# ScalarE's order at the end of an attention batch: two value chunks taken ahead of a weight unit's high half

## The chip, the core and the metric

The program runs on one core of a Trainium2 chip. The metric is device time in microseconds (us) of one execution. The core has TensorE (PE, with its weight loads shown apart as PEld), VectorE (DVE), ScalarE (ACT), GpSimd (POOL) and SyncE (SP), each with its own queue of instructions that runs in order and waits on semaphores. In the profile, PEclk is the TensorE clock that was granted, where 1.00 is 2.4 GHz and 0.50 is 1.2 GHz.

## The reference

For 4 batches of 512 tokens of width 256: layer norm, one attention head of width 256 over a context of 512 rows of width 192, a residual; then layer norm, a router that picks 2 of 8 experts per token, and a residual.

```
x = x + xattn(layernorm(x), ctx, Wq, bq, Wk, bk, Wv, bv)      # softmax(q k^T / 16) v
x = x + ffn(layernorm(x), Wr, W1, b1, W2, b2)
# ffn: probs = softmax(x Wr^T); the top 2 of 8, renormalised to w
#      out += (gelu(x W1[e]^T + b1[e]) W2[e]^T + b2[e]) * w_e      for each expert e
```

## The kernel before

The kernel has an attention phase, up to about 138 us, and an expert phase behind it, in which PE is busy nearly all the time with fp16 matmuls. The experts' fp32 weights are 16 units (W1 and W2 of 8 experts). They are loaded and split into a high and a low fp16 half during the attention phase, in the gaps of its engines. For each unit `u` the steps are:

- SP loads it into one of the staging buffers (`load_unit`, line 368). For a buffer that was used before, it first waits for the low half of the earlier unit (line 372).
- ACT squares it and sums it up (`square`, 852, the instruction is line 856). PE adds the sums over partitions (`add_all`, 691), two units at a time.
- DVE makes the scale factors out of that sum (`scale`, 1097: the first instruction, line 1105, reads the sum's PSUM bank and frees it, line 1112 writes `up`).
- ACT writes the high half (`high`, 859, line 861, 128x2048 elements). It waits for the factors (`scale_ready`).
- DVE writes the low half out of the staged unit and the high half (`low`, 1116, line 1121, two instructions of 128x1024). It waits for the high half (`high_ready`).

The attention of a batch `b` goes in four tiles of 128 queries: scores on PE (line 637) into `s_ps`, negated row maximum on DVE (`row_max`, line 1079), exponential on ACT (line 841), a transpose on PE (line 647) that ACT takes to SBUF (line 849), the product with the values on PE (`attend`, line 656), the residual on DVE (line 1092).

Projections and the small matmuls of the router share two PSUM banks, `proj0` and `proj1`, in a fixed order of uses (`projection_order`, line 111). Use n goes to bank n % 2, and PE waits in `begin` (line 571) until use n - 2 was taken. At the end of a batch the uses are the sum of two units (`sum`, taken by DVE's line 1105), and then the four chunks of the next batch's values (`v` 0 to 3, two matmuls each, shown as four), taken by ACT at line 832. So chunk 1 needs the bank of the sum, chunk 2 that of chunk 0, and chunk 3 that of chunk 1.

The order of the work is written by hand, engine by engine. At the end of batch b, with u = 4b, it reads (b from 0 to 2):

- PE: `attend(b, 2)`, the sum, `attend(b, 3)`, the four value chunks, then for batch b+1 `scores` 0 and 1, the sum of units u+4 and u+5, the transposes of `xn2` (`turn_normal`, line 611, two banks, the second of which waits until DVE has read that sum), the transpose of the first probabilities, `scores` 2, the logits.
- ACT: `square(u + 4)`, `high(u + 2)`, `values(b + 1)`, `high(u + 3)`, the store, `square(u + 5)`, then the first two exponentials of batch b+1.
- DVE (from line 1339): `scale(2b + 1)`, the last residual, the moments of the second layer norm (lines 1021, 1024), `low(u + 2)`, in batch 2 a table of 16 small instructions (`first_table`, 1194), `ln2_apply(b)` (line 1028), `rows_high` (line 1069), then for batch b+1 `row_max` 0, half of `low(u + 3)`, `row_max` 1, `scale(2b + 2)`.
- POOL: four indirect DMAs (line 516) that scatter rows of batch b-1, then the power that gives `rstd` for `ln2_apply` (line 503), then four more such DMAs.

Of the kernel before, what the change touches and what calls it, by code (L numbers as in the profile page):

```python
# [36 lines left out]
KT = LK // P  # L37
# [105 lines left out]
def build(nc, x, ctxT, WqT, bq, WkT, WvB, WrT, W1T, b1, W2T, b2, rows, out):  # L143
    uses = projection_order()
    with ExitStack() as ctx:
# [198 lines left out]
        def bank_of(*use):  # L344
            return proj[uses[use] % 2]

        def unit_tiles(u):

            e = u // 2
            return (w1h[:, e, :], w1l[:, e, :]) if u % 2 == 0 else (w2h[:, e, :], w2l[:, e, :])  # L350
# [471 lines left out]
        def _(act):  # L822
# [3 lines left out]
            def take(use, out_ap, in_ap, bias=None, scale=1.0):  # L826
                n = uses[use]
                if taken_by_vector(use):
                    return
                act.wait_ge(proj_full, n + 1)  # L830
                if bias is None:
                    nc.scalar.activation(out_ap, in_ap, ACT.Copy, scale=scale).then_inc(proj_free[n % 2], 1)
                else:
                    nc.scalar.activation(out_ap, in_ap, ACT.Identity, bias=bias, scale=scale).then_inc(proj_free[n % 2], 1)

            def soft(b, q):
                n = QT * b + q
                act.wait_ge(max_ready, n + 1)
                if n >= 2:
                    act.wait_ge(t_full, n - 1)  # L840
                nc.scalar.activation(probs[:, n % 2, :], s_ps[n % 2][:, 0:LK], ACT.Exp, bias=negmax[:, n:n + 1],
                                     accum_out=rowsum[:, n:n + 1]).then_inc(p_ready, 1)

            def take_turned(b, q):
                n = QT * b + q
                act.wait_ge(t_full, n + 1)
                if n >= 2:
                    act.wait_ge(o_full, n - 1)
                nc.scalar.activation(probsT[:, n % 2, :, :].rearrange("p a b -> p (a b)"), t_ps[n % 2][:],
                                     ACT.Copy).then_inc(pt_ready, 1)  # L850

            def square(u):


                act.wait_ge(staged_in[STAGE[u]], 16 * STAGE[0:u + 1].count(STAGE[u]))
                nc.scalar.activation(unit_tiles(u)[u < UNITS - 1].bitcast(BF16), stages[STAGE[u]], ACT.Square,
                                     accum_out=sq[:, u, 0:1]).then_inc(squared, 1)

            def high(u):
                act.wait_ge(scale_ready, u // 2 + 1)  # L860
                nc.scalar.activation(unit_tiles(u)[0], stages[STAGE[u]], ACT.Copy,
                                     scale=up[:, u, 0:1].bitcast(F32)).then_inc(high_ready, 1)
# [2 lines left out]
                for c in range(DC):  # L865
                    take(("a", 0, c), a_sb[:, c, 0:FEAT], bank_of("a", 0, c)[:, 0:FEAT])

            def values(b):
                for k in range(KT):
                    take(("v", b, k), v_sb[:, k, :], bank_of("v", b, k)[:, 0:D])  # L870

            def queries(b):
                for c in range(2):
                    take(("q", b, c), qT[0:PART[c], c, :], bank_of("q", b, c)[0:PART[c], 0:LQ],
                         bias=qb_sb[0:PART[c], c:c + 1], scale=SCALE)

            def turned_rows(name, b):
                for c in range(DC):
                    take((name, b, c), normT[:, c, :], bank_of(name, b, c)[:])

            def store(b):

                act.wait_ge(x2_ready, QT * (b + 1))
                if b:
                    act.wait_ge(stored, 16 * b)
                act.dma_start(out[b * LQ:(b + 1) * LQ, :].rearrange("(t p) d -> p t d", p=P),
                              x_sb[b % XBUF]).then_inc(stored, 16)

            def take_logits(b):
                take(("logits", b, 0), lg[:].rearrange("p a b -> p (a b)"), bank_of("logits", b, 0)[:, 0:QT * E])  # L890
# [8 lines left out]
            for b in range(B):  # L899
                u = QT * b  # L900
                last = b == B - 1
                soft(b, 0)
                if not b:
                    high(0)
                soft(b, 1)
                if b:
                    turned_rows("x2t", b - 1)
                take_turned(b, 0)
                if last:
                    square(u + 2)  # L910
                elif b:
                    high(u)
                else:
                    high(1)
                if b:
                    take_logits(b - 1)
                soft(b, 2)
                take_turned(b, 1)
                if last:

                    act.wait_ge(xn_ready, B)
                    act.wait_ge(proj_full, uses["xt", B - 1, 1] + 1)
                    square(u + 3)
                else:
                    square(u + 2)
                if b and not last:
                    high(u + 1)
                soft(b, 3)
                if not last:
                    turned_rows("xt", b + 1)  # L930
                take_turned(b, 2)
                if not last:
                    square(u + 3)
                    queries(b + 1)
                else:
                    high(u)
                take_turned(b, 3)
                if last:
                    high(u + 1)

                    act.wait_ge(stored, 16 * (B - 1))
                else:
                    square(u + 4)
                high(u + 2)
                if not last:
                    values(b + 1)
                high(u + 3)
                store(b)
                if not last:
                    square(u + 5)  # L950
# [529 lines left out]
```

## Time and profile before

| what | value |
|---|---|
| median of 3 runs | 376.73 us (376.52 to 377.44) |
| span of the profiled execution, first to last instruction | 373.9 us |
| PE, DVE, ACT, POOL busy | 336.9, 272.9, 189.5, 122.7 us |
| mean granted TensorE clock | 0.973 |

The profile gives the span of its execution and no other time of it; the median of the runs is 2.8 us above the span, for what lies ahead of the first and behind the last instruction. A busy share says how long an engine had work under way, and not whether the end of the kernel waited for it. For that there is the chain of waits, which is followed back from the last instruction. In the timeline a row is a start, a duration, an engine, a line and what is written out of what; "x8" is a count of merged instructions, and the bracket at its end is the engine's idle time before the row, with what ended it.

### The profile page before, as it was taken

What the parts mean: (1) busy time and instruction counts of PE and PEld (TensorE: products, weight loads), DVE (VectorE), ACT (ScalarE), POOL (GpSimd) and SP (SyncE); (2) the same over time, 40 slices, a digit from 0 to 9 for tenths busy, and PEclk for the clock granted to TensorE, in tenths of its full rate; (3) what the DMA queues carried; (4) which work ended last, traced back from release to release, by engine and by line L of the source; (5) the groups of instructions that cost most, each with busy time, mean ns of one, the idle gap of its engine ahead of it and who ended that gap; (6) DMA issues with size and microseconds to landing.
All of it is one profiled execution on the core that took longest, in us unless ns stands there. A gap on an engine that the chain in (4) does not pass through costs nothing.

```text
span 373.9 us, 8773 instructions
## 1 busy us (share of the span) xinstructions
PE 336.9 (90%) x2657; PEld 271.2 (73%) x2657; DVE 272.9 (73%) x753; ACT 189.5 (51%) x333; POOL 122.7 (33%) x124
## 2 busy tenths in 40 slices
PE   8998999789977849898699999999999999999980
PEld 4555765557645638787488888889898889988860
DVE  4259788987998699988777776756577776757760
ACT  2587798578577766171333334434454443445300
POOL 5017102382182173027623212233423132241322
PEclk9999999999989999999699999999999999999996
DMA  7977871465357326223425333434234333434312
GB/s 258 365 267 234 305 257 66 141 238 173 127 178 239 104 84 203 43 33 116 83 32 87 54 48 44 58 44 59 39 51 56 48 45 59 58 42 54 37 16 28
DMA packets 51112, 41.82 MB, mean 112 GB/s; under 512 B 28541, under 2 KB 46526, under 8 KB 50942
## 3 DMA queue, kind: packets, MB, share of 16 engines
q1 hardware_dynamic: 40798, 27.36, 26.0%
q0 software_dynamic: 7872, 11.77, 17.3%
q10 hardware_dynamic: 2400, 2.13, 1.7%
q8 instruction: 26, 0.43, 0.5%
q14 instruction: 16, 0.13, 0.1%
HBM read 22.28 MB, written 13.86 MB: 97 GB/s over the span
## 4 chain that ended last, share of the span: by engine, by line
PE 71%; DVE 16%; issue 5%; POOL 3%; ACT 1%; DMA 1%; POOLq 1%; DVEq 0%; SPq 0%; ACTq 0%
PE o_ps L781 26%; PE s_ps L763 15%; PE t_ps L763 13%; PE s_ps L637 3%; PE proj L624 3%; PE o_ps L656 3%; DVE w2l L1121 2%; DVE w1l L1121 2%; POOL rstd L503 2%; PE proj L603 2%; DVE negmax L1079 2%; PE o_ps L570 1%; PE proj L611 1%; POOL rows L516 1%; PE t_ps L647 1%
## 5 line engine op out<-in xcount | busy, mean ns | idle before, releaser
L548 POOL DMA_INDIRECT out<-y,xm x39 | 61.3, 1573 | 129.3 <-DVE y L1392 122.5
L969 ACT ACTIVATE g<-s_ps,b_sb,down 128x256 f32<-128x256 f32 (+1 forms) x100 | 45.4, 519 | 82.7 <-PE s_ps L763 72.2
L781 PE MATMUL o_ps<-w2h,gh 128*128 x312 | 85.0, 272 | 0.0
L781 PE MATMUL o_ps<-w2h,gl 128*128 x312 | 85.0, 272 | 0.0
L781 PE MATMUL o_ps<-w2l,gh 128*128 x312 | 85.0, 272 | 0.0
L1365 DVE TENSOR_SCALAR gh<-g,up 128x512 f16<-128x512 f32 x78 | 38.2, 489 | 36.5 <-ACT g L969 33.6
L969 ACT ACTIVATE g<-t_ps,b_sb,down 128x256 f32<-128x256 f32 (+1 forms) x92 | 42.3, 524 | 39.0 <-PE t_ps L763 38.6
L1367 DVE SCALAR_TENSOR_TENSOR gl<-g,up,gh 128x512 f16<-128x512 f32 x78 | 58.6, 752 | 2.8
L763 PE MATMUL s_ps<-xT,w1h 128*128 128x256 f16 (+1 forms) x400 | 52.3, 256 | 7.3 <-DVE w2l L1121 4.9
L763 PE MATMUL t_ps<-xT,w1h 128*128 128x256 f16 (+1 forms) x368 | 50.2, 261 | 0.8 <-issue 0.8
L516 POOL DMA_INDIRECT rows<-send,place x32 | 35.6, 1112 | 32.9 <-DVE place L1186 24.6
L763 PEld LDWEIGHTS s_ps<-xT,w1h 128*128 x400 | 35.0, 100 | 12.0 <-issue 8.6
L763 PEld LDWEIGHTS t_ps<-xT,w1h 128*128 x368 | 32.9, 100 | 7.0 <-issue 2.5
L763 PE MATMUL s_ps<-xT,w1l 128*128 128x256 f16 (+1 forms) x200 | 35.0, 256 | 2.9 <-issue 2.9
L781 PEld LDWEIGHTS o_ps<-w2h,gh 128*128 128x128 f16 x312 | 30.5, 98 | 4.4 <-issue 0.2
L781 PEld LDWEIGHTS o_ps<-w2l,gh 128*128 128x128 f16 x312 | 30.5, 98 | 3.8
L781 PEld LDWEIGHTS o_ps<-w2h,gl 128*128 128x128 f16 x312 | 30.5, 98 | 3.4
L763 PE MATMUL t_ps<-xT,w1l 128*128 128x256 f16 (+1 forms) x184 | 32.6, 259 | 0.0
L656 PE MATMUL o_ps<-v_sb,probsT 128*128 128x256 f32 x128 | 30.5, 383 | 0.0
L1388 DVE SCALAR_TENSOR_TENSOR y<-o_ps,undo,b_sb 128x256 f32<-128x256 f32 x39 | 18.9, 484 | 15.1 <-PE o_ps L781 8.6
L503 POOL TENSOR_TENSOR rstd<-vare,half 128x4 f32<-128x4 f32 x8 | 10.6, 1328 | 44.9 <-DVE vare L1024 44.9
L656 PEld LDWEIGHTS o_ps<-v_sb,probsT 128*128 128x128 f32 x128 | 23.1, 190 | 2.6
(231 smaller groups left out, 505.6 us busy)
## 6 DMA issues: line engine op xcount, KB each, us to landing
staged<-W2T SPq DMA_DIRECT2D x8, 1024.0 KB, 6.8
staged<-W1T SPq DMA_DIRECT2D x7, 1024.0 KB, 4.9
rows<-send POOLq DMA_DIRECT2D x8, 260.0 KB, 4.0
x_own<-x SPq DMA_DIRECT2D x2, 512.0 KB, 5.4
w2l<-W1T SPq DMA_DIRECT2D x1, 1024.0 KB, 10.3
out<-x_own ACTq DMA_DIRECT2D x2, 512.0 KB
b_sb<-b SPq DMA_DIRECT2D x1, 1024.0 KB, 5.5
out<-y,xm POOLq DMA_INDIRECT x39, 3.8
```

Of the source, the lines that this page charges most:

```text
L503: nc.gpsimd.tensor_tensor(rstd[:, which, b * QT:(b + 1) * QT], vare[:, which, b * QT:(b + 1) * QT], half[:, b * QT:(b + 1) * QT], ALU.pow) ...
L516: pool.indirect_dma_start(out=rows, out_offset=bass.IndirectOffsetOnAxis(ap=place[:, b, k, q:q + 1], axis=0), in_=send[b % 2][:, q, :], in ...
L548: pool.indirect_dma_start(out=out, out_offset=bass.IndirectOffsetOnAxis(ap=xm[:, t % MB, r, META - 1:META].bitcast(I32), axis=0), in_=y2[: ...
L624: i = nc.tensor.matmul(bank[0:PART[c], 0:LQ], a_sb[:, t, c * P:c * P + PART[c]], normT[:, t, :], start=(t == 0), stop=(t == DC - 1))
L656: i = nc.tensor.matmul(o_ps[n % 2][:, 0:D], probsT[:, n % 2, k, :], v_sb[:, k, :], start=(k == 0), stop=(k == KT - 1))
L763: i = nc.tensor.matmul(h_ps[group % 4][:, to:to + width(t)], w[:, bass.ds(e, 1), at:at + P].rearrange("p a n -> p (a n)"), xT[:, t % XB, x ...
L781: i = nc.tensor.matmul(y_ps[n % 2][:, 0:D], l[:, t % 2, m, r * P:(r + 1) * P], w[:, bass.ds(e, 1), m * D:(m + 1) * D].rearrange("p a n -> ...
L969: i = nc.scalar.activation(g[:, m, 0:width(t)], h_ps[group % 4][:, at:at + width(t)], ACT.Gelu, bias=b1_sb[:, bass.ds(e, 1), m:m + 1].rear ...
L1121: i = nc.vector.scalar_tensor_tensor(out=lo[:, n], in0=stages[STAGE[u]][:, n], scalar=up[:, u, 0:1].bitcast(F32), in1=hi[:, n], op0=ALU.mu ...
L1365: nc.vector.tensor_scalar(gh[:, t % 2, m, n], g[:, m, n], by, None, ALU.mult).then_inc(g_high, 1)
L1367: nc.vector.scalar_tensor_tensor(out=gl[:, t % 2, m, n], in0=g[:, m, n], scalar=by, in1=gh[:, t % 2, m, n], op0=ALU.mult, op1=ALU.subtract ...
L1388: nc.vector.scalar_tensor_tensor(out=y1[:, r, :], in0=y_ps[(BEFORE[t] + r) % 2][:, 0:D], scalar=undo[:, bass.ds(e, 1)], in1=b2_sb[:, bass. ...
```

## The change

ACT takes chunks 0 and 1 of the next batch's values ahead of `high(u + 2)`, and chunks 2 and 3 behind it, where all four stood behind it. That is at the end of batches 0, 1 and 2. No instruction is added or removed, and the orders of PE, DVE, POOL and SP stay as they are.

```
-            def values(b):
-                for k in range(KT):
+            def values(b, chunks):
+                for k in chunks:
                     take(("v", b, k), v_sb[:, k, :], bank_of("v", b, k)[:, 0:D])
...
                 else:
                     square(u + 4)
+                if not last:
+                    values(b + 1, range(0, 2))
                 high(u + 2)
                 if not last:
-                    values(b + 1)
+                    values(b + 1, range(2, KT))
                 high(u + 3)
                 store(b)
```

ScalarE's instructions at the end of batch 0, before (-) and now (+). `v_sb` holds the values, `w1h` is the high half of unit 2, `w2h` that of unit 3, and the line with `sq` is `square(4)`:

```order
 L849 ACTIVATE probsT<-t_ps 128x512
 L856 ACTIVATE w1l,sq<-w2l 128x2048
-L861 ACTIVATE w1h<-staged,up 128x2048
-L832 ACTIVATE v_sb<-proj 128x256 x4
+L832 ACTIVATE v_sb<-proj 128x256 x2
+L861 ACTIVATE w1h<-staged,up 128x2048
+L832 ACTIVATE v_sb<-proj 128x256 x2
 L861 ACTIVATE w2h<-staged,up 128x2048
 L886 DMA out<-x_own 128x4x256
```

Two of the four takes moved ahead of the high half of unit 2.

ScalarE's instructions at the end of batch 2, where `w1h` is the high half of unit 10, `w2h` that of unit 11, and the line with `sq` is `square(12)`:

```order
 L849 ACTIVATE probsT<-t_ps 128x512
 L856 ACTIVATE w1l,sq<-staged 128x2048
-L861 ACTIVATE w1h<-staged,up 128x2048
-L832 ACTIVATE v_sb<-proj 128x256 x4
+L832 ACTIVATE v_sb<-proj 128x256 x2
+L861 ACTIVATE w1h<-staged,up 128x2048
+L832 ACTIVATE v_sb<-proj 128x256 x2
 L861 ACTIVATE w2h<-staged,up 128x2048
 L886 DMA out<-w1h 128x4x256
```

The same two takes moved; at the end of batch 1 it is the same again.

## Rows read from the trace of the kernel before

**Rows 1.** The page: the chain that ended last, share of the span by engine.
```profile
PE 71%; DVE 16%; issue 5%; POOL 3%; ACT 1%; DMA 1%; POOLq 1%; DVEq 0%; SPq 0%; ACTq 0%
```

**Rows 2.** Timeline, end of batch 0, ACT and PE.
```profile
40.76 1.90 PE L603 MATMUL proj<-w1l,w2l 128*128 128x256 f32 x8
40.80 2.00 ACT L861 ACTIVATE w1h<-staged,up 128x2048 f16<-128x2048 f32 x1 [0.90 <-DVE up L1112]
...
42.71 0.64 ACT L832 ACTIVATE v_sb<-proj 128x256 f32<-128x256 f32 x2
...
43.12 2.00 PE L603 MATMUL proj<-w1l,w2l 128*128 128x256 f32 x8 [0.47 <-ACT v_sb L832]
44.29 0.38 ACT L832 ACTIVATE v_sb<-proj 128x256 f32<-128x256 f32 x1 [0.95 <-PE proj L603]
```

**Rows 3.** Timeline, end of batch 0, DVE.
```profile
42.83 2.48 DVE L1121 SCALAR_TENSOR_TENSOR w1l<-staged,up,w1h 128x1024 f16<-128x1024 f32 x2 [0.20 <-ACT w1h L861]
45.23 1.38 DVE L1028 TENSOR_SCALAR xn<-x_own,mv,rstd 128x256 f32<-128x256 f32 x4
...
49.05 0.68 DVE L1079 TENSOR_REDUCE negmax<-s_ps 128x1 f32<-128x512 f32 x1
49.80 0.16 DVE L1105 COPY total<-proj 128x4 f32<-128x4 f32 x1
```

**Rows 4.** Chain in order of time, first scores of batch 1: start, us, what.
```profile
50.69 0.44 PE t_ps L647 x4
51.13 1.73 PE s_ps L637 x4
```

**Rows 5.** Timeline, end of batch 1.
```profile
71.58 1.13 PE L603 MATMUL proj<-w1l,w1h 128*128 128x256 f32 x4 [0.39 <-DVE total L1105]
...
74.27 2.48 DVE L1121 SCALAR_TENSOR_TENSOR w1l<-staged,up,w1h 128x1024 f16<-128x1024 f32 x2
74.56 2.00 PE L603 MATMUL proj<-w1l,w1h 128*128 128x256 f32 x8 [1.85 <-issue]
74.67 1.72 POOL L516 DMA_INDIRECT rows<-send,place  x1 [0.30 <-issue]
...
76.40 1.25 POOL L503 TENSOR_TENSOR rstd<-vare,half 128x4 f32<-128x4 f32 x1
...
77.69 1.41 DVE L1028 TENSOR_SCALAR xn<-w2h,mv,rstd 128x256 f32<-128x256 f32 x4 [0.94 <-POOL rstd L503]
```

**Rows 6.** Timeline, end of batch 2.
```profile
103.92 1.13 PE L603 MATMUL proj<-w1l,w2l 128*128 128x256 f32 x4 [0.39 <-DVE total L1105]
...
104.61 2.00 ACT L861 ACTIVATE w1h<-staged,up 128x2048 f16<-128x2048 f32 x1
...
105.65 0.96 POOL L516 DMA_INDIRECT rows<-send,place  x1 [0.30 <-issue]
...
106.65 2.48 DVE L1121 SCALAR_TENSOR_TENSOR w1l<-staged,up,w1h 128x1024 f16<-128x1024 f32 x2
...
106.94 3.11 PE L603 MATMUL proj<-w1l,w2l 128*128 128x256 f32 x8 [1.89 <-issue]
...
109.84 4.22 PE L637 MATMUL s_ps<-w2l,qT 128*128 128x512 f32 x8
...
116.83 0.66 PE L611 MATMUL proj<-ident,xn 128*128 128x128 f32 x4 [1.66 <-DVE total L1105]
```

**Rows 7.** Windows: stretch, its length, each engine's busy time, PEclk, DMA.
```profile
103.53:107.68 4.15, 1.87 (x7) 1.36 (x8) 3.81 (x16) 3.63 (x5) 3.24 (x4) 1.00 0.77 277
107.68:111.09 3.41, 3.41 (x8) 2.36 (x7) 3.10 (x14) 1.39 (x3) 3.19 (x3) 0.50 0.28 56
...
116.83:125.31 8.48, 8.48 (x46) 6.30 (x47) 4.72 (x12) 6.10 (x12) 0.00 (x0) 1.00 0.45 140
133.20:138.16 4.96, 0.02 (x1) 0.00 (x1) 4.85 (x9) 2.86 (x2) 4.04 (x4) 1.00 0.21 75
138.40:141.81 3.41, 3.41 (x34) 3.38 (x33) 3.31 (x9) 1.49 (x2) 2.71 (x3) 0.50 0.72 242
```

## The prediction

> **What bounds the kernel now.** I read the page's chain first. PE holds 71% of it and DVE 16% [rows 1], but that is a mean over two phases, and the change lies in the first, the attention phase up to 138 us. So I read the chain in order of time there, and then the timeline at the ends of batches 0, 1 and 2. The reader is to look at who waits for whom at these three places.
>
> At the end of batch 0, PE waits 0.47 us at chunk 2 of the values until ACT has taken chunk 0, which stands behind the high half of unit 2 [rows 2]. At the end of batches 1 and 2 the same wait is 1.85 and 1.89 us [rows 5, 6]. The page calls these two "issue"; the order of the code names the take of chunk 0 as what PE lacks. These are the waits that the change takes away, 4.2 us in all. What matters is whether PE's next work, the scores of the new batch, is late for anybody.
>
> It is not. The scores go to DVE's row maximum, and DVE's own queue has in front of it the low half, the layer norm and the cast. At the end of batch 0 DVE starts the low half at 42.83, the moment ACT's high half lets it (it had waited 0.20), the layer norm at 45.23, the row maximum of tile 1 at 49.05 and the read of the sum at 49.80 [rows 3]. After the read PE goes on with the second transpose bank, the turned probabilities and scores 2 [rows 4]. At the end of batch 2 it is plainer still: PE waits 1.66 us for DVE's read of the sum [rows 6]. At the end of batch 1 DVE waits 0.94 us for POOL's rstd [rows 5]. So behind each boundary the end is set by DVE's queue, and in that queue the low half waits for exactly the instruction of ACT that the change puts later.
>
> **The change part by part.** Nothing is added or removed; two takes of the values are moved ahead of `high(u + 2)`, three times. What is behind the moved pair on ACT is the high half, and behind it on other engines are DVE's low half with all of DVE's queue, and SP's load that waits for the low half. That load is a buffer's next unit, squared many instructions later, and I cost it at nothing; if it came late, ACT's square would wait as many us as it is late.
>
> End of batch 0. PE's eight value instructions of chunks 0 and 1 start at 40.76 and end at 42.66. A take starts about 0.17 behind its chunk's end: chunk 2 starts at 43.12, ends half of 2.00 later at 44.12, and is taken at 44.29 [rows 2]. So chunk 1 is taken at 42.8. Two takes last 0.64 and one 0.38, so the next instruction starts 0.3 behind it: the high half starts at 43.1 instead of 40.80, 2.3 us later. It ends at 45.1, and DVE starts the low half at 45.1 instead of 42.83. Everything up to the read of the sum is back to back on DVE. That read has a slack of 0.07 (49.05 + 0.68 = 49.73, start 49.80) to 0.2, since instructions on DVE can start a little ahead of the end of the former one. The cost is 2.1, between 2.0 and 2.3.
>
> End of batch 1. Chunk 1's matmuls start at 71.58, held by DVE's read of the sum, and end at 72.7; the take is at 72.9 and the high half at 73.1. Before, the high half ran up to the start of the low half at 74.27, so it started at about 72.25: 0.9 later. The low half then starts at 75.1, and DVE is free 2.40 behind it (45.23 - 42.83, rows 3), at 77.5. Before, DVE stood idle until rstd at 77.69 [rows 5]. The cover of 0.94 holds the 0.9.
>
> The last scatter of POOL ahead of rstd took 1.72 us, beside a low half that had started 0.4 before it [rows 5]; one with DVE's low half a microsecond away took 0.96 [rows 6]. With the low half at 75.1, the scatter at 74.67 starts with DVE quiet. If it then takes about 1.0, rstd starts at 75.7 and, held up until the first of the low half's two instructions ends at 76.3, is done at 77.3; the layer norm starts at 77.5, a gain of 0.2. If the scatter is held up all the same, it ends 0.9 behind 76.3, rstd is held by the second instruction until 77.6 and done at 78.5, a loss of 0.8. I take a gain of 0.1, with both ends kept.
>
> The Trainium skill (GPSIMD Engine Reference, section Key points) says that GpSimd shares its SBUF interfaces with VectorE and contends with VectorE instructions that have two SBUF inputs. The low half is of that kind, and the 1.72 against 0.96 us agrees. By that rule the sum is as it stands; without it the term would be 0 instead of -0.1.
>
> End of batch 2. Chunk 1's matmuls start at 103.92 and end at 105.05; the take is at 105.2, the high half at 105.4 instead of 104.61 [rows 6]. DVE starts the low half at 106.65, right behind the high half, and from there to the read of the sum it has no gap, as the wait of PE for that read shows. The cost is 0.8, between 0.7 and 1.0.
>
> The order alone gives 2.1 - 0.1 + 0.8 = 2.8 us. PE's 4.2 us of waits are gone, but PE has them back at once as a longer wait for the sum: at the end of batch 0 the scores are done at the latest by 48.5 (chunk 3 at 44.2, then 4.2 even at the half rate of rows 6) and DVE reads the sum at 51.9.
>
> That longer wait brings the second term, the granted clock. In 103.53 to 107.68, where PE was busy 1.87 of 4.15 us, the clock was 1.00; then it fell to 0.50 for the next 3.41 us. After 0.02 busy in 133.20 to 138.16 it fell again for 3.41 us [rows 7]. At 107.68 the fall cost nothing, since PE only ran scores for which DVE was not ready. In the changed kernel the thin stretches lie just ahead of PE work that is on the path. At the end of batch 2, PE is done with the scores at 110.5 and gets the sum's read at 117.6: some 7 us with about 1 us of work (the small sum and four transposes at 0.66). That is thinner than either stretch of rows 7 in length or in share, and I take a fall there as nearly sure. Behind it the path is PE alone, 8.48 busy of 8.48 us [rows 7], so 3.41 us at half rate cost half of that, 1.7 (between 0.8, if half of it is over before the read, and 3.4, if it came twice).
>
> At the ends of batches 0 and 1 the thin stretch is about 4.5 us with 1 us of work, near the one of rows 7 that brought a fall (1.87 of 4.15). But the 1.85 us wait at the end of batch 1 brought none, so I give each 6 in 10. PE is on the path there for the second bank (0.66), the probabilities (0.44) and scores 2 (1.73) [rows 4, 6], 2.8 us, before DVE has the chain again. A fall costs 0 to 2.8, and I take 1.2 for one, as part of it lies in the wait. The term: one of these two and the third, 1.2 + 1.7 = 2.9.
>
> The Trainium skill (TensorE: Matmul & The Clock Gate, section HAM oscillation — how this bites in real kernels) warns that idle gaps put PE back to the throttled rate and that each burst behind such a gap starts slow. It speaks against this change, which joins short waits to long ones. The trace agrees in 133.20 to 138.16 and behind it.
>
> The sum is 2.8 + 2.9 = 5.7 us on top of the span of 373.9, so 379.6. The runs' median is 2.8 above the span and nothing in the change touches that part: 376.7 + 5.7 = 382.4.
>
> **The rivals.** First, PE's waits decide: the 0.47, 1.85 and 1.89 us come off the end, and the time is 376.7 - 4.2 = 372.5. For it speaks that PE holds 71% of the chain. Against it speaks that DVE's read of the sum is late for PE already, 1.66 us at the end of batch 2 [rows 6]. It would decide only if DVE's low half did not have to wait for the high half.
>
> Second, the order's cost alone: the clock stays up, or falls where PE waits anyway. Then it is 376.7 + 2.8 = 379.5. For it: the wait of 1.85 us at the end of batch 1 left the clock at 1.00.
>
> Third, the clock falls at all three and at a high price: 2.8 + 2 x 2.3 + 1.7 = 9.1, so 385.8.
>
> Fourth, the delay is absorbed. A later wait for a load, or for something else that does not move with DVE, would eat it, and the time stays at 376.7. For it would speak a wait of DVE or PE on a DMA behind the boundaries. But the loads of units wait for low halves, so they move with DVE.
>
> **How the numbers follow.** The forecast's own case has a chance of 0.52, the order alone 0.20, three dear falls 0.12, PE's waits 0.08, absorbed 0.08. Case by case, the range of the forecast's case is 380.5 to 384.5. To leave no more than 2 in 10 outside, the range goes from 378.3, where the order costs its least and half is absorbed, to 385.3. About 0.3% (1.1 us) is what a measurement of this kernel can tell from no change. Faster by more has 0.08 (the first rival), within it 0.08 (the fourth), slower 0.84 (the other three).
>
> **What would show it.** In the changed kernel's timeline, PE's values of four chunks should stand without a wait of over 0.4 us, and the scores of batches 1, 2 and 3 start 1 to 3 us earlier against the end of the former batch. DVE should wait before the low half of unit 2 by 2.3 us more, and of unit 10 by 0.8 more. PE's wait for DVE's read of the sum should be longer at all three places, above all in batch 3, and the row maximum of tile 2 should come later by 2.1 in batch 1. The windows should show 0.50 in the stretch behind the last of these waits. I am wrong if the chain behind the ends of batches 0 and 2 does not go through DVE's low half, or if the scores turn out to be what DVE waited for.

## The result and the profile after

The changed kernel takes 384.77 us (median of 4 runs, 384.13 to 385.28), the kernel before in the same comparison 376.62 (376.09 to 377.44): a ratio of 1.0219, 95% interval 1.0198 to 1.0239. It is 8.15 us slower, where 5.7 was forecast. Its profiled execution has a span of 382.9 us against 373.9, and a mean granted clock of 0.956 against 0.973. Medians and ranges hold all runs of a kernel, while ratios and their intervals leave out those more than 1.5% above its quickest, here and in the experiments.

In every run of which both are known, the time is 1.7 to 1.9 us above the span. So the profile of before, with its 373.9 us, is of an execution of some 375.7 us (an estimate from that difference), about 0.9 below its median of 376.62. The 2.8 us between the median and that span are not all time outside the span, and the two profiles lie further apart (9.0 us) than the medians (8.15).

The chain of the page, by engine, answers to [rows 1]:

```profile
PE 72%; DVE 14%; issue 4%; ACT 2%; DMA 2%; POOL 2%; POOLq 0%; ACTq 0%; SPq 0%; another core or an unknown queue 0%; DVEq 0%
```

It says almost nothing: the shares move by a point or two, and the 9 us are inside them. The three places have to be read. In all rows of the changed kernel the line numbers behind the diff are 2 higher (L1105, DVE's read of the sum, is L1107).

The timeline of the changed kernel at the end of batch 0 (start, us, engine, line, operation, count, [idle before <- what ended it]):

```profile
41.45 3.63 PE L603 MATMUL proj<-w1l,w2l 128*128 128x256 f32 x16
43.67 1.99 ACT L861 ACTIVATE w1h<-staged,up 128x2048 f16<-128x2048 f32 x1
45.69 2.48 DVE L1123 SCALAR_TENSOR_TENSOR w1l<-staged,up,w1h 128x1024 f16<-128x1024 f32 x2 [2.37 <-ACT w1h L861]
...
50.04 0.38 PE L695 MATMUL proj<-sq,ones 128*128 128x4 f32 x2 [1.52 <-ACT w2l L856]
...
52.50 0.15 DVE L1107 COPY total<-proj 128x4 f32<-128x4 f32 x1
52.71 1.11 PE L611 MATMUL proj<-ident,xn 128*128 128x128 f32 x4 [1.79 <-DVE total L1107]
...
54.47 2.43 PE L637 MATMUL s_ps<-w2l,qT 128*128 128x512 f32 x4
56.94 0.69 DVE L1081 TENSOR_REDUCE negmax<-s_ps 128x1 f32<-128x512 f32 x1 [2.22 <-PE s_ps L637]
```

All four chunks of the values are now one group of 16 matmuls without a wait: the 0.47 us of [rows 2] are gone. The high half starts at 43.67 instead of 40.80, DVE waits 2.37 us for it instead of 0.20 [rows 3], and its queue runs on back to back to the read of the sum at 52.50. PE waits 1.79 us for that read, where the kernel before shows no wait. The sum itself, which hangs on ACT's square, is ready at 50.42 (50.04 + 0.38), 2.1 us ahead of the read: it is DVE that is late, and not ACT's later instructions. Then come the transposes at 1.11 us, which take 0.66 in [rows 6], and the row maximum of tile 2 waits 2.22 us for its scores. In the kernel before the same row maximum waits 0.86:

```profile
52.88 0.69 DVE L1079 TENSOR_REDUCE negmax<-s_ps 128x1 f32<-128x512 f32 x1 [0.86 <-PE s_ps L637]
```

The end of batch 1 in the changed kernel, which answers to [rows 5]:

```profile
75.64 2.87 PE L603 MATMUL proj<-w1l,w1h 128*128 128x256 f32 x12 [0.39 <-DVE total L1107]
...
78.73 0.96 POOL L516 DMA_INDIRECT rows<-send,place  x1 [0.30 <-issue]
79.11 2.48 DVE L1123 SCALAR_TENSOR_TENSOR w1l<-staged,up,w1h 128x1024 f16<-128x1024 f32 x2 [0.71 <-ACT w1h L861]
79.72 1.58 POOL L503 TENSOR_TENSOR rstd<-vare,half 128x4 f32<-128x4 f32 x1
81.51 1.43 DVE L1030 TENSOR_SCALAR xn<-w2h,mv,rstd 128x256 f32<-128x256 f32 x4
...
86.18 1.06 PE L611 MATMUL proj<-ident,xn 128*128 128x128 f32 x4 [1.84 <-DVE total L1107]
87.89 2.78 PE L637 MATMUL s_ps<-w1h,qT 128*128 128x512 f32 x4
90.71 0.69 DVE L1081 TENSOR_REDUCE negmax<-s_ps 128x1 f32<-128x512 f32 x1 [2.52 <-PE s_ps L637]
```

And the end of batch 2, which answers to [rows 6]:

```profile
109.46 3.01 PE L603 MATMUL proj<-w1l,w2l 128*128 128x256 f32 x12 [0.39 <-DVE total L1107]
110.91 1.99 ACT L861 ACTIVATE w1h<-staged,up 128x2048 f16<-128x2048 f32 x1
...
112.93 2.48 DVE L1123 SCALAR_TENSOR_TENSOR w1l<-staged,up,w1h 128x1024 f16<-128x1024 f32 x2 [0.81 <-ACT w1h L861]
...
123.19 1.11 PE L611 MATMUL proj<-ident,xn 128*128 128x128 f32 x4 [2.43 <-DVE total L1107]
124.95 3.03 PE L637 MATMUL s_ps<-w2l,qT 128*128 128x512 f32 x4
128.02 0.69 DVE L1081 TENSOR_REDUCE negmax<-s_ps 128x1 f32<-128x512 f32 x1 [2.81 <-PE s_ps L637]
```

At both places PE's wait of 1.85 and 1.89 us inside the values is gone, and the wait for the sum's read at the end of batch 2 has grown from 1.66 to 2.43. The windows of the changed kernel around the three places (stretch, length, busy time of PE, PEld, DVE, ACT and POOL, PEclk, DMA share, GB/s) answer to [rows 7]:

```profile
47.00:52.71 5.71, 2.40 (x10) 1.02 (x9) 5.64 (x11) 3.85 (x6) 0.00 (x0) 0.95 0.72 235
52.16:55.57 3.41, 2.86 (x10) 2.34 (x11) 2.42 (x8) 2.69 (x6) 0.00 (x0) 0.50 0.16 54
86.29:89.70 3.41, 3.41 (x11) 2.37 (x12) 1.80 (x6) 3.15 (x6) 0.05 (x1) 0.50 0.84 282
115.91:123.19 7.28, 1.14 (x6) 0.72 (x6) 6.80 (x26) 2.18 (x5) 3.33 (x4) 0.81 0.67 217
120.42:127.25 6.83, 4.40 (x14) 2.77 (x12) 4.65 (x11) 4.67 (x8) 0.00 (x0) 0.50 0.20 74
```

PE was busy 2.40 of 5.71 us and 1.14 of 7.28 us ahead of the read, and the clock went to half at all three places: 0.55 us ahead of the work that the read lets go at batch 0 (52.16 against 52.71), 0.11 behind its start at batch 1 (86.29 against 86.18), and 2.77 ahead of it at batch 2 (120.42 against 123.19), where it lasted 6.83 us and so reached into that work too.

To see where the 9 us lie, I subtracted the start of each DVE instruction in the profile of before from that of the same instruction after; there are 753 in both, in the same order. The difference grows at few places. "Start-up" is what it has gained by the first attention tile, ahead of any changed instruction, and "rest" what it gains from the first expert tile on. "Order" is what it gains at one boundary up to the read of the sum, "clock" what it gains from there to the end of the half-rate stretch. This splits by place and not by cause: half rate ahead of the read would be counted as "order". In the changed kernel the clock was 1.00 up to 0.34 us before the read at batch 0 and all the way at batch 1, and at batch 2 DVE, which sets that read, has no wait for PE; so there the split by place is also one by cause.

| kernel | start-up | batch 0 order, clock | batch 1 order, clock | batch 2 order, clock | rest | all |
|---|---|---|---|---|---|---|
| changed | 0.69 | 2.02, 1.36 | -0.22, 1.69 | 0.82, 1.98 | 0.56 | 8.91 |

The order costs 2.62 us and the clock 5.03. The other 1.25 us lie in the first loads, before any changed instruction (0.69), and in the experts (0.56).

### The profile page after: what moved, and what is told of

Same layout as the page of the kernel before. It is cut to its first block, busy times and chain, and to the rows that moved or that the text cites. A ratio compares the mean times of both kernels' runs of the same rounds, so it can differ in the third digit from the quotient of the medians.

```text
span 382.9 us, 8772 instructions
## 1 busy us (share of the span) xinstructions
PE 340.7 (89%) x2656; PEld 274.2 (72%) x2657; DVE 272.8 (71%) x753; ACT 190.1 (50%) x333; POOL 120.9 (32%) x124
## 4 chain that ended last, share of the span: by engine, by line
PE 72%; DVE 14%; issue 4%; ACT 2%; DMA 2%; POOL 2%; POOLq 0%; ACTq 0%; SPq 0%; another core or an unknown queue 0%; DVEq 0%
PE o_ps L781 26%; PE s_ps L763 14%; PE t_ps L763 13%; PE o_ps L656 5%; PE s_ps L637 4%; PE proj L624 4%; PE proj L603 2%; PE proj L611 2%; DVE w1l L1123 2%; DVE negmax L1081 2%; PE t_ps L647 2%; DVE w2l L1123 2%; ACT w1h L861 1%; DMA w1h<-WkT 1%; POOL rstd L503 1%
## 5 line engine op out<-in xcount | busy, mean ns | idle before, releaser
L763 PE MATMUL s_ps<-xT,w1h 128*128 128x256 f16 (+1 forms) x400 | 53.1, 258 | 9.6 <-DVE w2l L1123 4.9
L516 POOL DMA_INDIRECT rows<-send,place x32 | 32.9, 1027 | 32.9 <-DVE place L1188 24.6
L503 POOL TENSOR_TENSOR rstd<-vare,half 128x4 f32<-128x4 f32 x8 | 11.4, 1423 | 51.9 <-DVE vare L1026 51.8
```

The source lines that it names most:

```text
L516: pool.indirect_dma_start(out=rows, out_offset=bass.IndirectOffsetOnAxis(ap=place[:, b, k, q:q + 1], axis=0), in_=send[b % 2][:, q, :], in ...
L763: i = nc.tensor.matmul(h_ps[group % 4][:, to:to + width(t)], w[:, bass.ds(e, 1), at:at + P].rearrange("p a n -> p (a n)"), xT[:, t % XB, x ...
```

## The experiments

Each profile was put through the same subtraction. Times are compared with the kernel before, run beside them: its median was 377.35 us beside "batch 0 only", "batch 1 only", "batch 1, one chunk" and the first "changed, PE kept busy"; 377.77 beside the second profile of the changed kernel, "batch 2 only", "batch 0, layer norm first" and "before, PE busy ahead of the experts"; and 373.52 beside the other four.

| kernel | start-up | batch 0 order, clock | batch 1 order, clock | batch 2 order, clock | rest | all |
|---|---|---|---|---|---|---|
| changed, second profile | 0.85 | 2.01, 4.73 | -0.21, 5.06 | 0.81, 1.57 | 0.34 | 15.16 |
| batch 0 only | 0.37 | 2.02, 1.60 | 0.27, 0.00 | 0, 0.01 | -1.22 | 3.07 |
| batch 1 only | 0.57 | 0, 0 | -0.21, 4.79 | 0, 0 | 0.31 | 5.47 |
| batch 2 only | 0.51 | 0, 0.01 | 0, 0 | 0.81, 1.72 | 0.41 | 3.46 |
| batch 1, one chunk | 0.72 | 0, 0.01 | 0, 0 | 0.01, 0.01 | 0.17 | 0.92 |
| batch 0, layer norm first | 0.53 | 0.67, 1.67 | 0.27, 0 | 0, 0 | -0.28 | 2.87 |
| changed, PE kept busy | 0.64 | 2.02, -0.03 | -0.21, 0 | 0.81, 0.32 | -0.25 | 3.30 |
| the same, second profile | 0.98 | 2.02, -0.03 | -0.21, 0 | 0.81, 1.52 | -2.89 | 2.21 |
| before, PE kept busy | 0.26 | 0, 1.29 | 0.79, 1.33 | 0, 0 | -3.69 | -0.02 |
| before, PE busy ahead of the experts | 0.19 | 0, 0.01 | 1.53, 0.01 | 0.01, 0 | -0.71 | 1.04 |
| before, rstd first | 1.30 | 0, 0 | 0.26, 0 | 0.20, 6.14 | -3.10 | 4.82 |
| the same, PE kept busy | 0.88 | 0, 0.43 | -0.90, 0.46 | 0.20, 6.28 | -2.90 | 4.46 |

The last group of four is the quickest: its kernels all have a rest of about -3 us, and its kernel before is some 4 us quicker than in the other groups, though the second and the last group ran on a chip of the same number. So "all" can't be compared across groups, while the terms at the boundaries can.

Some terms need reading with care, since half rate ahead of the read stands under "order". The 0.27 at batch 1 in "batch 0 only" and "layer norm first", and the 1.53 in "before, PE busy ahead of the experts", stand at a boundary whose code is that of the kernel before, and each has a fall of the clock in PE's wait inside the values or just behind it. The dearest of them:

```profile
74.75 3.78 PE L603 MATMUL proj<-w1l,w1h 128*128 128x256 f32 x8 [1.85 <-issue]
...
81.46 0.69 DVE L1081 TENSOR_REDUCE negmax<-s_ps 128x1 f32<-128x512 f32 x1 [1.44 <-PE s_ps L637]
```

The clock was 0.50 from 73.93 to 80.76 there; the values took 3.78 us instead of 2.00 [rows 5]. So the wait of 1.85 us is not safe in the kernel before: of the five profiles with this boundary unchanged (before, "batch 0 only", "batch 2 only", "layer norm first", and the one above) three have a fall there, at 0.27, 0.27 and 1.53 us. At the end of batch 0 the six unchanged profiles have none, and at the end of batch 2 the six with both the order and GpSimd's queue unchanged and no added matmuls there each have one that costs 0.00 or 0.01. The 0.26 in "rstd first" and a part of the 0.79 in "before, PE kept busy" are of the same kind, and are read below.

**The change at one boundary alone.** Three kernels take two chunks first at the end of batch 0, 1 or 2 only. For batch 0 (`b == 1` and `b == 2` in the others):

```diff
+                early = 2 if b == 0 else 0
                 if not last:
-                    values(b + 1, range(0, 2))
+                    values(b + 1, range(0, early))
                 high(u + 2)
                 if not last:
-                    values(b + 1, range(2, KT))
+                    values(b + 1, range(early, KT))
```

> The new order of ScalarE at the end of batch 0 alone; batches 1 and 2 as before. Theory (VectorE's low half waits for the delayed high half, and the joined waits of TensorE bring a fall of the granted clock on the path): slower than before by 2.0 us for the order plus 1.3 us for one fall, 3.3 us in all (2.0 if the clock doesn't fall). Rival (TensorE's removed waits matter): faster by up to 0.5 us.

> The new order at the end of batch 1 alone. Theory: the order gives back 0.2 us, since VectorE waited for GpSimd's rstd anyway, and a fall of the clock ahead of scores 2 of batch 2 costs 1.3 to 2.1 us: slower by 1.1 to 1.9 us. If the clock doesn't fall, faster by 0.2 us. Rival (the 1.85 us wait that goes is worth its length): faster by 1.8 us.

> The new order at the end of batch 2 alone. Theory: 0.8 us for the later high half of unit 10 and 1.4 to 2.1 us for a fall of the clock ahead of scores 2 of batch 3: slower by 2.2 to 2.9 us. Rival (TensorE's wait of 1.89 us is worth its length): faster by 1.1 us.

Measured: 380.44 us (378.56 to 380.95), ratio 1.0094 [1.0066, 1.0123] for batch 0; 380.45 (377.62 to 383.82), 1.0057 [1.0023, 1.0092] for batch 1; 383.13 (379.18 to 385.23), 1.0172 [1.0130, 1.0214] for batch 2. At the changed boundaries the order terms are those of the changed kernel to 0.01 us, so they add up; the 0.27 elsewhere is the clock's, as said. Each boundary also brings its own fall of the clock on the path. The forecasts were 3.3 us for batch 0 (its profile gives 2.02 + 1.60, its ratio 3.5), 1.1 to 1.9 for batch 1 (4.79 - 0.21 in its profile, 2.2 by its ratio) and 2.2 to 2.9 for batch 2 (2.53 in its profile, more by its times). None is faster, so PE's removed waits are worth nothing that shows. The windows of half rate in "batch 1 only" and "batch 2 only":

```profile
81.37:95.02 13.65, 12.32 (x39) 9.63 (x40) 8.34 (x25) 8.16 (x15) 3.12 (x3) 0.50 0.57 184
```
```profile
114.86:121.69 6.83, 4.64 (x15) 3.21 (x16) 5.14 (x12) 4.14 (x8) 0.27 (x1) 0.50 0.26 101
```

In the first, half rate lasts 13.65 us and costs 4.79; in the changed kernel's first profile the same fall lasted 3.41 and cost 1.69. The twelve times of "batch 1 only" fit that: the five of 377.62 to 378.96 us have a mean clock of 0.960 to 0.964, the seven of 379.78 to 383.82 us one of 0.947 to 0.950. The order's gain of 0.2 at batch 1 is therefore not worth having: the kernel is slower with it. The timed +1.72% of batch 2 (6.5 us; its median is 5.4 us higher) is more than its profile's 0.81 + 1.72, but that profile is of its quickest run (379.18, mean clock 0.964); the others have 0.940 to 0.955. Longer half rate would fit, and was not profiled: this part of its loss is open.

**One chunk first, batch 1 only.** `early = 1 if b == 1 else 0`, all else as above.

> Only chunk 0 is taken ahead of the high half, at the end of batch 1 alone. ScalarE is idle at that time and chunk 0 is ready 0.5 us before the scale factors, so no high or low half comes later. Theory (order and clock are separate costs): the order costs 0.0 (VectorE and the chain unchanged), TensorE's wait of 1.85 us moves behind the scores, the clock falls there and costs 1.3 to 2.1 us. Rival (all of the loss comes from the later high half): no change, within 0.3 us of before.

Measured: 378.87 us (376.31 to 383.99), 1.0042 [1.0013, 1.0071]. The timeline of this kernel, PE and ACT:

```profile
71.94 0.38 ACT L832 ACTIVATE v_sb<-proj 128x256 f32<-128x256 f32 x1 [2.21 <-PE proj L603]
72.96 2.00 ACT L861 ACTIVATE w1h<-staged,up 128x2048 f16<-128x2048 f32 x1 [0.63 <-DVE up L1115]
...
75.28 1.13 PE L603 MATMUL proj<-w1l,w1h 128*128 128x256 f32 x4 [0.98 <-issue]
...
83.07 0.66 PE L611 MATMUL proj<-ident,xn 128*128 128x128 f32 x4 [1.52 <-DVE total L1108]
84.00 1.89 PE L637 MATMUL s_ps<-w1h,qT 128*128 128x512 f32 x4
```

I had expected PE's wait to go behind the scores. It stays inside the values, at chunk 3, which needs the take of chunk 1: 0.98 us instead of 1.85. The transposes take 0.66 and the scores 1.89, both at full rate, and nothing is lost here. So neither the theory (1.3 to 2.1 us for a fall) nor its rival was put to the test, since the wait did not move. The timed 0.4% is not in this profile (376.72 us, within the runs of before); I leave it open.

**The layer norm ahead of the low half, batch 0.** If the low half in DVE's queue is what turns ACT's delay into time, then something of DVE's that doesn't need the high half, put ahead of it, should cover part of the delay. "Batch 0 only" and:

```diff
-                    low(u + 2)
+                    if b:
+                        low(u + 2)
                     if b == B - 2:
                         first_table()
                     ln2_apply(b)
+                    if not b:
+                        low(u + 2)
```

> The new order of ScalarE at the end of batch 0 alone, and VectorE does the second layer norm of batch 0 ahead of the low half of unit 2 and not behind it. Theory (the cost at this place is VectorE's wait for the high half): the layer norm fills 1.4 us of the wait, so the read of the sum comes 1.0 us later than in the kernel before, where it comes 2.0 us later with ScalarE's order alone; the clock may fall as there. Rival (the cost comes from what ScalarE does later, its squares and exponentials): no better than with ScalarE's order alone.

Its DVE timeline:

```profile
44.32 1.38 DVE L1031 TENSOR_SCALAR xn<-x_own,mv,rstd 128x256 f32<-128x256 f32 x4 [1.16 <-POOL rstd L503]
45.61 2.48 DVE L1124 SCALAR_TENSOR_TENSOR w1l<-staged,up,w1h 128x1024 f16<-128x1024 f32 x2
...
51.00 0.16 DVE L1108 COPY total<-proj 128x4 f32<-128x4 f32 x1
```

DVE's 2.37 us of waiting became 1.16, for POOL's rstd, and the order cost at the end of batch 0 fell from 2.02 to 0.67 us (1.0 expected). The fall of the clock stayed and cost 1.67. Its time was 383.18 us (376.31 to 384.00, 6 runs), so it is no faster than "batch 0 only" (380.44). The gain is shown for the order term in one profile (378.62 us) alone; what made the slower runs slow was not profiled.

**The changed kernel once more.** No edit; a second profile.

> The changed kernel once more, beside the kernel before on the same chip, as the measure for the dummy matmuls. Theory: slower by 2.6 us for the order and by 3.5 to 5.1 us for the clock, 6 to 8 us in all. Rival: if the clock is not part of it, slower by 2.6 us only.

Measured: 386.52 us (385.79 to 390.86), 1.0252 [1.0224, 1.0280]. By the ratio that is 9.5 us, more than the 6 to 8 expected, and far from the rival's 2.6. The profiled run is the slowest, 390.86. Its windows:

```profile
51.39:65.04 13.65, 12.17 (x39) 9.57 (x40) 8.48 (x25) 8.15 (x15) 1.91 (x1) 0.50 0.44 158
88.93:102.59 13.66, 12.88 (x41) 10.08 (x42) 7.79 (x25) 8.49 (x13) 2.87 (x2) 0.50 0.50 165
```

The order terms repeat to 0.01 us. The clock term is 11.36 us instead of 5.03, because two of the three falls lasted 13.65 us. So in these two profiles the order's cost is the same, and the clock's is what varies.

**PE kept busy through the waits.** The direct test of the clock term: matmuls on a constant tile into a bank that nobody reads, 5 ahead of the sum's matmuls, once the last x2 of the former batch is there, and 6 between the two banks of transposes, ahead of PE's wait for DVE's read of the sum (`begin` stands behind them). The output is the same. Both in the changed kernel and in the one before:

```diff
                 for c in range(DC):
+                    if name == "x2t" and c == 1 and b + 1 < B:
+                        keep_warm(6)
                     bank = begin((name, b, c))
...
                 if b:
+                    pe.wait_ge(x2_ready, QT * b)
+                    keep_warm(5)
                     add_all(2 * b)
```

> The changed kernel with 5 dummy matmuls of 128x512 bf16 on TensorE ahead of the sum of batches 1, 2 and 3, and 6 more ahead of the second bank of the transposes in the same batches, all in its waits. Theory: the clock stays up behind the first two boundaries, which gives back 1.35 + 1.69 us, and perhaps behind the third (2.05 us): 2.7 to 5.1 us faster than the changed kernel, 379.5 to 382 us. Rival (scores 2 is slow for another reason, such as what VectorE and ScalarE do at the same time): no faster than the changed kernel, 384.8 us or more.

> The kernel before with the same dummy matmuls (5 ahead of the sum, 6 ahead of the second bank of the transposes). Theory: the waits they fill are shorter here (0.81 and 0.65 us at the end of batch 1, none at the second place of batch 1's start), so they delay TensorE by up to 1 us per batch and save no fall: slower than before by 1 to 3 us. Rival (the dummy matmuls speed up any kernel, and what they did for the changed one says nothing of its waits): faster than before by over 0.5 us.

Changed kernel with them: 379.65 us (378.44 to 381.14), 1.0084 [1.0051, 1.0116], within the 379.5 to 382 of the theory. The PE timeline and the windows at the end of batch 0:

```profile
48.31 1.24 PE L702 MATMUL o_ps<-busy 128*128 128x512 bf16 x5
...
50.70 1.46 PE L702 MATMUL o_ps<-busy 128*128 128x512 bf16 x6
52.66 0.66 PE L613 MATMUL proj<-ident,xn 128*128 128x128 f32 x4 [0.51 <-DVE total L1111]
...
53.59 1.88 PE L639 MATMUL s_ps<-w2l,qT 128*128 128x512 f32 x4
```
```profile
47.00:52.70 5.70, 4.76 (x22) 2.09 (x20) 5.63 (x11) 3.84 (x6) 0.00 (x0) 1.00 0.65 217
52.70:57.00 4.30, 4.30 (x28) 3.34 (x29) 3.35 (x10) 4.00 (x6) 0.00 (x0) 1.00 0.32 68
```

And its DVE timeline, the row maxima that waited 2.22 and 2.52 us:

```profile
55.52 0.69 DVE L1085 TENSOR_REDUCE negmax<-s_ps 128x1 f32<-128x512 f32 x1 [0.84 <-PE s_ps L639]
...
87.61 0.69 DVE L1085 TENSOR_REDUCE negmax<-s_ps 128x1 f32<-128x512 f32 x1 [0.84 <-PE s_ps L639]
```

Busy 4.76 of 5.70 us instead of 2.40 of 5.71, PE keeps the clock at 1.00. The transposes take 0.66 again instead of 1.11, the row maximum waits 0.84, and the clock terms of batches 0 and 1 are -0.03 and 0.00. The order terms are untouched. This settles the second term at batches 0 and 1: it was the clock, and PE's idle time ahead of the read was what brought the fall. At batch 2 the added matmuls didn't hold it: half rate for 3.41 us cost 0.32, and in the second profile, for 6.83 us, 1.52.

The rival was that the added matmuls help for another reason, and would help the kernel before as well. They don't: 376.51 us (375.10 to 377.94) with them against 373.52, 1.0089 [1.0059, 1.0119]. By the table they cost 1.29 us at batch 0, where they stand in PE's way, and 0.79 and 1.33 at batch 1, where the clock also fell once (3.41 us from 77.23; 0.26 of the 0.79 is DVE waiting for scores at half rate). The kernels of the two orders, on one chip:

> The changed kernel with the dummy matmuls once more, on this chip. Theory: slower than before by 2.6 us for the order alone, up to 3.2 with a part of a fall in batch 3, as against 8.2 to 8.7 us without the dummies. Rival: within 1 us of the changed kernel's loss.

Measured: 376.23 us (374.49 to 378.64), 1.0081 [1.0051, 1.0110], 2.7 us above before by the medians and 3.0 by the ratio: the order's cost and a part of a fall, as the theory has it, and not the 8 us of the changed kernel. That the two kernels with these matmuls come out alike (1.0089 and 1.0081) does not mean that the order is free: the changed one pays 2.62 us for its order, and the one before pays 3.4 (1.29 + 0.79 + 1.33) for matmuls that stand in PE's way, with a fall. Neither is a version to use.

**Can the kernel before be made faster by the same reasoning?** In its profile the clock falls at the end of batch 2, where that costs nothing, at 138 us, at the first expert tile, at 179.35 us among the experts, for 6.83 us, and at the very end. Tried was the one at 138. 18 matmuls in the wait there:

```diff
             now = expert(0)
+            pe.wait_ge(pt_ready, QT * B)
+            keep_warm(18, t_ps[1])
             pe.wait_ge(low_ready, 2 * FIRST_E)
```

> The kernel before with 18 dummy matmuls of 128x512 bf16 on TensorE in its wait of 5 us ahead of the first expert tile. Theory (a fall of the clock costs half of its length where TensorE is on the path): the hidden matmuls of the first tile run at the full rate, 4.66 us in the chain become about 2.8, and the kernel is faster than before by 1 to 1.8 us. Rival (the work behind waits for ScalarE and VectorE anyway): within 0.5 us of before.

Measured: 377.74 us (375.72 to 382.76), 1.0001 [0.9977, 1.0024]. Its timeline at 138 us:

```profile
135.02 3.83 PE L700 MATMUL t_ps<-busy 128*128 128x512 bf16 x17
139.92 0.46 PE L763 MATMUL s_ps<-xT,w1h 128*128 128x128 f16 x4 [1.06 <-DVE w2l L1123]
...
144.98 2.90 ACT L971 ACTIVATE g<-s_ps,b_sb,down 128x128 f32<-128x128 f32 x8 [2.67 <-PE s_ps L763]
```

There was no fall at 138, and no gain: the first tile's 48 matmuls ran from 139.92 to 144.06, 4.1 us, at full rate, against 4.6 in the kernel before (138.16 to 142.72), where the clock was at half for 3.41 us. Six of them took 0.64 us at half rate and 0.48 at full, so "half rate costs half of its length", which the float32 scores bear out (1.88 us at full, 3.62 at half), is too much here. And the 0.4 us did not come through: the next group of matmuls (into `t_ps`) starts 5.00 us behind the first ones before (143.16) and 4.98 now (144.90), ACT's `g` 4.92 and 5.06. What they wait for the profile doesn't name.

The other cover to try is POOL's. rstd ahead of the last scatter of a batch lets DVE's layer norm of batch 1 start without the 0.94 us of [rows 5]:

```diff
-                    send_rows(b - 1, 0)
+                    send_rows(b - 1, 0, range(0, QT if last else 3))
                 if not last:
                     rsqrt(1, b, ln2_var, ln2_rstd)
                 if b:
+                    if not last:
+                        send_rows(b - 1, 0, range(3, QT))
                     send_rows(b - 1, 1)
```

> The kernel before, with GpSimd's power that gives rstd ahead of the fourth of the row scatters instead of behind it, in batches 1 and 2. ScalarE's order is the one before. Theory: at the end of batch 1 VectorE is free 0.9 us before rstd comes, and this removes that wait: faster by 0.9 to 1.0 us. At the end of batch 2 nothing. Rival (VectorE's table or the clock eats it): within 0.3 us.

The second has a few of the busy matmuls with it: 2 ahead of the sum, 2 ahead of the second bank, and 6 in the wait inside the values.

```diff
                 for k in chunks:
+                    if b >= 2 and k == 2:
+                        pe.wait_ge(x2_ready, QT * (b - 1) + 3)
+                        keep_warm(6)
```

> The same with 6 dummy matmuls ahead of chunk 2 of the values of batches 2 and 3, 2 ahead of the sum and 2 ahead of the second bank of the transposes. Theory: the waits of 1.85 and 1.89 us are filled, so no alignment of the clock costs anything there: faster than before by 1.0 to 1.5 us with less spread. Rival (the dummies delay work on the path): slower than the kernel without them.

Measured: 373.70 us (371.82 to 380.58), 1.0008 [0.9980, 1.0035], and 375.19 (373.30 to 380.08), 1.0048 [1.0014, 1.0083]. The first one's POOL and DVE timeline:

```profile
75.57 2.48 DVE L1123 SCALAR_TENSOR_TENSOR w1l<-staged,up,w1h 128x1024 f16<-128x1024 f32 x2
75.72 2.04 POOL L503 TENSOR_TENSOR rstd<-vare,half 128x4 f32<-128x4 f32 x1
77.97 1.43 DVE L1030 TENSOR_SCALAR xn<-w2h,mv,rstd 128x256 f32<-128x256 f32 x4
...
81.30 0.69 DVE L1081 TENSOR_REDUCE negmax<-s_ps 128x1 f32<-128x512 f32 x1 [1.17 <-PE s_ps L639]
```

The layer norm does start 1.05 us earlier against what precedes it, as expected, but then DVE waits 1.17 us for scores that PE runs at half rate (0.50 from 76.61 to 80.02): the clock ate the gain, as the rival has it. With the clock at 1.00 the gain stays. The kernel with the busy matmuls had no fall at this boundary, DVE did not wait for the scores, and the read of the sum came 0.90 us earlier than before:

```profile
80.05 0.68 DVE L1088 TENSOR_REDUCE negmax<-s_ps 128x1 f32<-128x512 f32 x1
...
82.54 0.16 DVE L1114 COPY total<-proj 128x4 f32<-128x4 f32 x1
```

By the table the same kernel lost 0.46 us behind that read and 0.43 at batch 0, where no fall was and the added matmuls are all that is new on PE, and both kernels had half rate for 13.65 us behind the end of batch 2 (6.14 and 6.28 us). These profiles are of two of the slowest runs (380.58 and 379.99 us), so only the places are read from them. In the timed medians neither beats the kernel before, and no other version tried does.

## Why the prediction was right, and where its sizes were off

The direction, the time (384.8 in 378.3 to 385.3) and both mechanisms hold. How near the edge it is was luck in part: 384.8 is above the 384.5 that the forecast gave its own case, the range's upper end of 385.3 stands without a sum and below the third rival's own 385.8, and the same kernel's second median, 386.52 (against a before of 377.77), would lie outside. Point by point:

- **Bound.** DVE's queue, led by the low half, sets the end of each batch. Shown three ways: the delay of the low half, 2.17 and 0.74 us, reappears at the read of the sum as 2.02 and 0.82 (the 0.08 more comes within the layer norm of batch 2), moving the layer norm ahead of the low half takes 1.35 of 2.02 us away, and PE's removed waits brought nothing, which is the first rival's fall. Nothing absorbed the delay either: no order term shrank at a later wait. The 0.15 that is missing at batch 0 is the slack that the prediction named: before, DVE was through with its row maximum at 49.73 and the sum was there at 49.76, so the read at 49.80 waited for PE as much as for DVE's queue.
- **End of batch 0**, 2.1 forecast: 2.02. **End of batch 1**, -0.1: -0.22. The scatter, which now starts 0.38 us ahead of the low half and not 0.40 behind its start, took 0.96 us instead of 1.72 [rows 5], and rstd, begun 0.6 behind the low half's start, 1.58. That is the gaining one of the two cases. **End of batch 2**, 0.8: 0.82. The sum of the order is 2.62 for 2.8.
- **The clock**, 2.9 forecast: 5.03, and 11.36 in the second profile. This is the step that was mis-sized, "one of these two and the third, 1.2 + 1.7 = 2.9". First, the sum counts one fall at the first two boundaries (6 in 10 each), and the clock fell at both, in both profiles of the changed kernel; the wait of 1.85 us without a fall in the one profile of before was a bad guide, as the falls at that same place in three of the later profiles show. "Batch 1, one chunk", with 0.98 us inside the values and 1.52 behind the scores, had no fall; "batch 1 only", with both chunks, had one. Second, one fall cost 1.4 to 2.0, near the 1.7 taken for the third, but for the first two I had marked it down to 1.2 as lying partly in the wait. Third, I took 3.41 us as the length, from the only two falls of [rows 7]; it was also 6.83 and 13.65. The profile of before has one of 6.83 us itself, from 179.35 among the experts, which was not read for this.
- **The third rival**, three falls at 385.8 us, is nearest to the measured 384.8. It had a chance of 0.12. Its price of 2.3 each for the first two was too high for the first profile (1.36, 1.69) and too low for the second (4.73, 5.06). The forecast's case and this rival differ in how often the clock falls and in the price of a fall, and I should have put them closer.
- **The remaining 1.25 us** of the profile's 8.91 belong to neither term. Up to 0.9 of them may come from the profile of before, which is of an execution quicker than its median. The start-up part lies in the loads (0.19 to 1.30 in the profiles of the experiments), before the first changed instruction, so it is not of the change; for the 0.56 in the experts nothing here names a cause. In both profiles of the changed kernel the half rate at the first expert tile lasts 6.83 us instead of 3.41, which lies in that part.

The predicted signs in the profile came out but for one: values without a wait over 0.4, DVE's wait at unit 2 longer by 2.17 and at unit 10 by 0.74, and 0.50 behind the last wait. PE's wait for the read grew at all three places, but not above all in batch 3: from 0 to 1.79, from 0.65 to 1.84 and from 1.66 to 2.43 us. The row maximum of tile 2 was later by 4.06 in absolute time: 2.02 of order, 1.36 of clock, 0.69 of start-up.

## What to carry to other kernels

Before moving work ahead of an instruction to fill an engine's gap, ask who starts on that instruction; if it is the engine whose queue sets the end, the gap was free and the delay is not, and its size can be read to 0.1 us from the rows. Then look at what the waits become: two short ones put together ahead of work on the path can cost more through the clock than the order itself. Price a fall at each such place with its length open, since the order's cost repeats to 0.01 us here and the clock's does not. And look for falls in more than one profile of the kernel before: one without a fall does not show that a wait is safe.

## What the runs showed of the hardware that was not expected

- In the 14 profiles the granted clock stayed at 0.50 for 3.41, 6.83 or 13.65 us behind a fall (the last one of each kernel, at its end, aside). In the longest, PE was busy 12.2 to 12.9 of 13.65 us and stayed at half rate. Seen at one attention boundary in "batch 1 only" and in both POOL kernels, and at two in the second profile of the changed kernel. Cost: 4.7 to 6.3 us each, against 1.4 to 2.0 for the shorter ones behind the changed order. What decides the length is open.
- A fall's price depends on the instructions behind it: four 128x512 float32 matmuls took 2.43 to 3.62 us instead of 1.88, by how much of them lay in the fall, and six float16 matmuls of 128 columns 0.64 instead of 0.48.
- What rstd on POOL takes depends on how its start lies to the low half of DVE. With DVE quiet it took 1.03 us (the changed kernel, 43.41), and the same when it began 0.11 us ahead of the low half (before, 42.73). Begun 0.6 behind the low half's start it took 1.58, begun 0.15 behind it 2.04: in "rstd first" at batch 1, POOL started at 75.72 and was done at 77.76, 0.3 before DVE's pair ended at 78.05. At batch 2 of that kernel it began 0.02 behind (108.24 against 108.22) and took 1.04. The Trainium skill (GPSIMD Engine Reference, section Key points) says that GpSimd contends with VectorE instructions of two SBUF inputs; the scatter at 0.96 us ahead of the low half and 1.72 begun beside one [rows 5] agrees, and so do the 1.58 and 2.04, while the two of 1.03 and 1.04, which also ran beside a low half, show no loss. Why a start just ahead or together is spared, no run here shows.
